# A Swin transformer block on one core: the first and last four steps ordered by hand, preparation and loads shared out anew

## The chip, the core and the metric

The kernel runs on one core of a Trainium2 chip. A core has five engines with an instruction queue of their own each: TensorE (PE, matrix products), VectorE (DVE), ScalarE (ACT), GpSimd (POOL) and SyncE (SP, here only for DMAs). They run side by side and wait for each other by semaphores. The metric is the device time of one execution in microseconds (us).

## What is computed

The reference is one Swin block on x of shape (32, 56, 56, 128) in float32: shifted windows of 7 x 7 tokens, 4 heads of 32, then an MLP with 512 hidden columns.

```python
h = roll(_ln(x, g1, b1), (-3, -3))            # then cut into windows of 49 tokens
q, k, v = split(h @ w_qkv + b_qkv)
attn = softmax(q * HD**-0.5 @ k.T + bias + MASK)
x = x + roll(window_reverse((attn @ v) @ w_proj + b_proj), (3, 3))
return x + gelu(_ln(x, g2, b2) @ w_fc1 + b_fc1) @ w_fc2 + b_fc2
```

## The kernel before

A step is 14 image rows: two bands of 8 windows, 784 tokens, held as 7 tiles of 112 tokens. An image has 4 steps, so there are 128 (`steps`). Tiles are handled in two halves, h = 0 (4 tiles) and h = 1 (3 tiles). The work of one step is spread over several turns of the loop: in turn n the kernel makes q and k of step n+1, attention and projection of step n, the hidden layer of step n-1 (`make_hidden`, 8 chunks, 0 to 3 for band 0 and 4 to 7 for band 1) and the output product of step n-2 (`make_out`).

The order is written out by hand: every engine has a function `step(n)` with its operations in a fixed order, and `run_steps` calls it for n from -3 to steps+1. `has(k)` leaves out the parts whose step does not exist, so the first and last turns keep the order of a full turn with holes in it. All waits are for semaphores that count steps.

What bears on the prediction:
- TensorE: `make_q`, `make_k`, `make_scores` (64 small products a band), `transpose_probs`, `attend`, `project`, `make_hidden` (L725 to L727, three passes), `make_out` (L767), `transpose_tiles` (L700).
- VectorE: `stats1`, `stats2`, `mean_var`, `normalise` (L530), `shift_scores` (L545 adds bias and mask, reading PSUM and writing the tile scores in SBUF; L548 takes the maximum; L550 subtracts it), `inverse_sums`, `add_to_stream` (L564: residual and final sum), `split_x` and `split_x2` (low parts).
- ScalarE: copies out of PSUM (`copy_q` L400, `copy_k`, `copy_x`, ...), `exp` (L361), `gelu` (L413). Exp and gelu need different tables, loaded by ACT_TABLE_LOAD; `load_gelu_table` (L417) loads the gelu table ahead of time with a probe of one column.
- GpSimd: `power` (rstd), `normalise_probs` (L313), `add_row` (L320: adds a bias row to the residual).
- SyncE: loads x four steps ahead, stores a step's result after both halves have their final sum.
- Preparation: weights are scaled by the layer norm's g and split in high and low parts on VectorE; TensorE makes the products of b with the weights. It is done before the first turn.

```python
283        def step(n):                                    # SyncE
290            if has(n - 2):
292                wait(sp, out_added[0], upto(n - 2))
293                wait(sp, out_added[1], upto(n - 2))
294                store((n - 2) // STEPS, (n - 2) % STEPS)
772        pe.wait_ge(front_loaded, 6 * 16)                # TensorE
```

## Time and profile before

| | us |
|---|---|
| median of 3 runs | 2976.29 (2975.44 to 2977.2) |
| the profiled execution | 2974.32 |
| its span, first to last instruction | 2972.7 |
| TensorE busy | 2932.2 (99%) |
| VectorE, ScalarE, GpSimd busy | 2578.3, 2260.8, 1299.7 |

A busy time is the sum of an engine's instructions. The granted clock is the share of full speed that TensorE had. In lists of rows, "x56" is a number of merged instructions, and "[5.03 <-DVE xn L530]" says that the engine stood idle 5.03 us before the row until that line of VectorE released it.

### The profile page before, as it was taken

Reading aid. Unit: us, or ns where it says so; the run is one execution under the profiler, and the core shown is the slowest. Engines: PE = TensorE matmul, PEld = TensorE weight load, DVE = VectorE, ACT = ScalarE, POOL = GpSimd, SP = SyncE. Lnnn points to the kernel's source line nnn. Section 1 sums busy time; section 2 is a strip of 40 time slices with the busy share of each in tenths; the row PEclk is TensorE's granted clock in tenths of the full one; section 3 lists DMA queues with packets and bytes.
Section 4 is the critical chain, followed back from the end, with each engine's and each line's share of the span. In section 5 each row is a group of like instructions: output and inputs, shape, how many; then the busy total and the mean of one; then the engine's idle time right before and its main releaser. Section 6 shows DMA issues by size and latency. Waiting matters only on the chain.

```text
span 2972.7 us, 119245 instructions
## 1 busy us (share of the span) xinstructions
PE 2932.2 (99%) x51984; PEld 2726.2 (92%) x51984; DVE 2578.3 (87%) x7463; ACT 2260.8 (76%) x4482; POOL 1299.7 (44%) x775
## 2 busy tenths in 40 slices
PE   6999999999999999999999999999999999999998
PEld 5999999999999999999999999999999999999997
DVE  7888888888888888888888888888888888888885
ACT  4777777777777777777777777777777777777775
POOL 3444444444444444444444444444444444444442
PEclk8999999999999999999999999999999999999999
DMA  2111111111111111111111111111111111111110
GB/s 52 41 35 40 35 40 35 40 37 38 37 38 40 35 40 36 41 35 40 35 40 35 40 36 40 36 39 40 35 39 37 40 35 40 35 40 35 40 24 23
DMA packets 217569, 111.77 MB, mean 38 GB/s; under 512 B 15094, under 2 KB 216790, under 8 KB 217046
## 3 DMA queue, kind: packets, MB, share of 16 engines
q1 hardware_dynamic: 215523, 103.16, 13.6%
q8 instruction: 406, 6.65, 1.0%
q10 hardware_dynamic: 1523, 1.01, 0.1%
q14 instruction: 117, 0.96, 0.1%
HBM read 52.73 MB, written 51.38 MB: 35 GB/s over the span
## 4 chain that ended last, share of the span: by engine, by line
PE 97%; DVE 2%; ACT 0%; POOL 0%; issue 0%; DMA 0%; SPq 0%; POOLq 0%; DVEq 0%
PE psum L767 26%; PE psum L725 10%; PE psum L727 8%; PE psum L726 8%; PE psum L693 7%; PE psum L746 7%; PE psum L708 7%; PE psum L753 7%; PE psum L700 6%; PE psum L732 6%; PE psum L720 6%; DVE xn L530 0%; ACT hT L413 0%; DVE row_max L548 0%; DVE scores L545 0%
## 5 line engine op out<-in xcount | busy, mean ns | idle before, releaser
L317 POOL TENSOR_TENSOR rstd<-ve,minus_half 112x7 f32<-112x7 f32 x256 | 381.1, 1489 | 1076.6 <-DVE ve L525 1076.6
L767 PEld LDWEIGHTS psum<-wfc,hT 128*112 128x112 f32 x7168 | 799.1, 177 | 38.9 <-issue 19.3
L767 PE MATMUL psum<-wfc,hT 128*112 128x128 f32 x7168 | 803.4, 273 | 1.4 <-ACT hT L413 1.4
L413 ACT ACTIVATE hT<-psum,bias_h 128x392 f32<-128x392 f32 x1024 | 575.5, 608 | 246.1 <-PE psum L727 246.1
L313 POOL TENSOR_TENSOR probs<-probs,row_inv 128x784 f32<-128x784 f32 x256 | 388.9, 1520 | 570.9 <-DVE row_inv L559 564.2
L564 DVE TENSOR_TENSOR stream<-psum,stream 112x512 f32<-112x512 f32 (+1 forms) x512 | 307.2, 609 | 204.2 <-PE psum L753 183.3
L725 PE MATMUL psum<-x2T_hi,wfc_hi 128*128 128x392 f32 x1024 | 397.2, 388 | 2.8 <-DVE x2T_lo L575 1.3
L727 PE MATMUL psum<-x2T_lo,wfc_hi 128*128 128x392 f32 x1024 | 349.3, 341 | 0.3 <-issue 0.3
L726 PE MATMUL psum<-x2T_hi,wfc_lo 128*128 128x392 f32 x1024 | 348.5, 340 | 0.1
L395 ACT ACTIVATE x2T_hi<-psum 128x336 fp32r<-128x336 f32 (+1 forms) x256 | 127.2, 497 | 254.8 <-PE psum L700 254.8
L400 ACT ACTIVATE qd<-psum,bias_q,parity_one 128x392 f32<-128x392 f32 x512 | 316.0, 667 | 5.8 <-PE psum L727 3.8
L700 PE MATMUL psum<-ident,xn 112*128 112x112 f32 x1792 | 264.6, 264 | 6.2 <-DVE xn L530 5.7
L320 POOL TENSOR_TENSOR stream<-x_in,brow_proj 112x896 f32<-112x896 f32 x128 | 269.6, 2106 | 0.0
L320 POOL TENSOR_TENSOR stream<-stream,brow_fc 112x896 f32<-112x896 f32 x128 | 268.3, 2096 | 2.0 <-DVE xn L530 2.0
L746 PE MATMUL psum<-wv,xT 128*113 128x128 f32 x2048 | 267.0, 274 | 0.0
L708 PEld LDWEIGHTS psum<-ident,probs 113*128 113x128 f32 x2048 | 218.4, 142 | 47.2 <-issue 23.6
L369 ACT ACTIVATE probsT<-psum 128x452 f32<-128x452 f32 x512 | 258.0, 572 | 0.8 <-PE psum L708 0.8
L550 DVE TENSOR_TENSOR scores<-scores,row_max 128x784 f32<-128x784 f32 x256 | 249.5, 975 | 8.7
L548 DVE TENSOR_REDUCE row_max<-scores 128x16 f32<-128x784 f32 x256 | 248.3, 970 | 8.8
L575 DVE TENSOR_TENSOR x2T_lo<-psum,x2T_hi 128x336 fp32r<-128x336 f32 (+1 forms) x256 | 143.6, 561 | 128.6 <-ACT x2T_hi L395 128.6
L746 PEld LDWEIGHTS psum<-wv,xT 128*113 128x113 f32 x2048 | 249.1, 178 | 0.0
L545 DVE TENSOR_TENSOR scores<-psum,bias_rel 128x784 f32<-128x784 f32 x256 | 246.1, 961 | 0.0
(78 smaller groups left out, 5707.3 us busy)
## 6 DMA issues: line engine op xcount, KB each, us to landing
x_in<-in_x SPq DMA_DIRECT2D x224, 168.0 KB
out<-stream SPq DMA_DIRECT2D x224, 168.0 KB
x_in<-in_x SPq DMA_DIRECT2D x224, 17.5 KB
out<-stream SPq DMA_DIRECT2D x224, 17.5 KB
x_in<-in_x SPq DMA_DIRECT2D x224, 10.5 KB
out<-stream SPq DMA_DIRECT2D x224, 10.5 KB
x_in<-in_x SPq DMA_DIRECT2D x32, 96.0 KB
out<-stream SPq DMA_DIRECT2D x32, 96.0 KB
```

Of the source, the lines that this page charges most:

```text
L313: pool.tensor_tensor(p, p, r.unsqueeze(2).to_broadcast([128, 2 * WINDOWS, N]), ALU.mult).then_inc(probs_normed[band], 1)
L317: pool.tensor_tensor(rstd[:, :], ve[:, :], minus_half[:, :], ALU.pow).then_inc(ready, 1)
L320: pool.tensor_tensor(stream[:, k % STEPS, :, :], src[:, k % STEPS, :, :], row[:, :].unsqueeze(1).to_broadcast([TOK, TILES, C]), ALU.add).t ...
L400: last = act.activation(qd[:, band, parity, :], qkvo_psum(Q_BANK[band])[:, 0:BAND], ACT.Identity, bias=bias_q[:, parity:parity + 1], scale ...
L413: act.activation(hT[:, chunk, band * BAND:(band + 1) * BAND], tok_psum(c)[:, 0:BAND], ACT.Gelu, bias=bias_h[:, chunk:chunk + 1]).then_inc( ...
L700: last = pe.transpose(tok_psum(h)[:, (t - t0) * TOK:(t - t0 + 1) * TOK], src[:, t, :], ident[0:TOK, 0:TOK])
L708: last = pe.transpose(psum[:, S_BANK + 2 * band + f, 128 * pair:128 * pair + rows], probs[0:rows, band, f, 2 * pair:2 * pair + 2, :].rearr ...
L725: pe.matmul(made, w_hi, x_hi, start=True, stop=False)
L726: pe.matmul(made, w_lo, x_hi, start=False, stop=False)
L727: return pe.matmul(made, w_hi, x_lo, start=False, stop=True)
L746: last = pe.matmul(qkvo_psum(V_BANK[band])[0:rows, pair * C:(pair + 1) * C], windows[:, 0:rows], wv[:, :], start=True, stop=True)
L767: last = pe.matmul(tok_psum(h)[0:TOK, (t - t0) * C:(t - t0 + 1) * C], hT[:, chunk, t * TOK:(t + 1) * TOK], wfc2[:, chunk, :], start=chunk ...
```

## The change

All `step(n)` functions, `has`, `fresh` and `run_steps` go. Each engine gets a straight list for steps 0 to 3, a loop `for n in range(4, steps - 4)` with the order of the old turn, and a straight list for the last four. In the new lists:
- SyncE loads x of step 0, the mask, half of the bias slices, x of step 1, then w_proj and b_proj, then x of steps 2 and 3. ScalarE's queue loads g1, b1, w_qkv, b_qkv first, then the other half of the slices, then the six MLP loads.
- GpSimd clears the padding columns of xT. VectorE clears only the padding of probs and 392 columns of the four score banks; both cleared whole tiles before.
- `make_bias_rel` is in two parts, the second behind step 3's first shift. The wfc1 split comes after `split_x(1, 1)`. The products of the biases go to banks of their own.
- `shift_scores` keeps the biased scores in PSUM, in all steps: the add writes the banks that it reads, maximum and subtraction read them.
- Scores of a step are made before the attention of the step ahead of it is finished, in the first and in the last steps.
- The last step is stored in four parts, each half as soon as its sum is there, band 0 by SyncE and band 1 by ScalarE's queue.

```diff
+        def store_last(eng, h, bands):
+            eng.wait_ge(out_added[h], steps)
+            for dst, src in token_pieces(STEPS - 1, out, images - 1, stream[:, STEPS - 1, :, :], *HALVES[h], bands):
+                eng.dma_start(dst, src).then_inc(out_stored[STEPS - 1], 16)
             load(0, 0)
-            for dst, src in ((wqkv[:, :], w_qkv), (vecs[:, 0:1], g1), (vecs[:, 1:2], b1), (bqkv[:, :], b_qkv),
-                             (wproj[:, :], w_proj), (brow_proj_in[:, :], b_proj.to_broadcast([TOK, C]))):
-                sp.dma_start(dst, src).then_inc(front_loaded, 16)
+            sp.dma_start(mask_sb[:, :, :, :], mask).then_inc(mask_loaded, 16)
             load_rel(sp, 0)
+            load(0, 1)
+            for dst, src in ((wproj[:, :], w_proj), (brow_proj_in[:, :], b_proj.to_broadcast([TOK, C]))):
+                sp.dma_start(dst, src).then_inc(proj_loaded, 16)
...
+            store_last(sp, 1, (0,))
+            store_last(sp, 0, (0,))
...
-                dve.tensor_tensor(sc, scores_psum(band), bias_rel[:, last_band, :, :, :].rearrange("p f w m -> p f (w m)"),
+                dve.tensor_tensor(made, made, bias_rel[:, last_band, :, :, :].rearrange("p f w m -> p f (w m)"),
                                   ALU.add).then_inc(scores_biased[band], 1)
...
-                dve.tensor_reduce(mx, rows, AX_X, ALU.max).then_inc(max_done[band], 1)
+                dve.tensor_reduce(mx, biased, AX_X, ALU.max).then_inc(max_done[band], 1)
...
-                dve.tensor_tensor(rows, rows, mx.unsqueeze(2).to_broadcast([128, 2 * WINDOWS, N]),
+                dve.tensor_tensor(scores[:, band, :, :, :], biased, mx.unsqueeze(3).to_broadcast([128, 2, WINDOWS, N]),
                                   ALU.subtract).then_inc(scores_shifted[band], 1)
```

TensorE's list begins:

```diff
+            make_qkv_biases()
+            pe.wait_ge(biases_ready, 1)
+            make_proj_bias()
+            pe.wait_ge(xn1_ready[0], 1)
+            transpose_tiles(xn1, 0, xT_made)
+            pe.wait_ge(xn1_ready[1], 1)
+            transpose_tiles(xn1, 1, xT_made)
+            make_hidden_biases()
...
+            make_scores(0)
...
+            make_k(0, 1)
+            make_values(0, 1)
+            pe.wait_ge(k_copied[1], 1)
+            make_k(1, 0)
+            pe.wait_ge(late_biases_ready, 1)
+            make_scores(1)
+            pe.wait_ge(k_copied[0], 2)
+            make_q(1, 0)
+            pe.wait_ge(q_copied[0], 2)
+            make_scores(0)
```

ScalarE's part up to the first exp, and VectorE's behind step 0's softmax:

```diff
+            copy_k(1)
+            act.wait_ge(k_made[0], 2)
+            copy_k(0)
+            load_gelu_table()
+            act.wait_ge(scores_shifted[0], 1)
+            exp(0)
+            act.wait_ge(q_made[0], 2)
+            copy_q(0)
...
+            inverse_sums(0, 1)
+            dve.wait_ge(scores_made[0], 2)
+            shift_scores(1, 0)
+            copy_v()
+            normalise(xn1, x_in[:, (2) % STEPS, :, :], mean1, rstd1, xn1_ready, 0)
```

TensorE's list ends, from the scores of the last step on (shortened):

```diff
+            make_scores(1)
...
+            make_hidden(2)
...
+            make_hidden(7)
+            make_values(steps - 1, 0)
...
+            make_out(0)
+            make_out(1)
...
+            attend(1)
+            pe.wait_ge(gelu_done[5], steps - 1)
+            make_hidden(7)
+            pe.wait_ge(o_copied[0], steps)
+            project(0)
+            pe.wait_ge(gelu_done[7], steps - 1)
+            project(1)
+            pe.wait_ge(residual_added[0], steps)
+            make_hidden(2)
+            pe.wait_ge(residual_added[1], steps)
+            make_out(1)
+            pe.wait_ge(gelu_done[2], steps - 1)
+            make_out(0)
...
+            make_hidden(2)
+            pe.wait_ge(gelu_done[7], steps)
+            make_out(1)
+            pe.wait_ge(gelu_done[2], steps)
+            make_out(0)
```

## Rows read from the trace of the kernel before

**Rows 1.** Stretches: length, each engine's busy time, granted clock, DMA share, GB/s.

```profile
0.00:25.00 25.00, 9.84 (x35) 6.66 (x39) 19.91 (x89) 5.94 (x12) 4.42 (x10) 1.00 0.50 118
25.00:50.00 25.00, 17.93 (x359) 15.48 (x363) 17.04 (x38) 14.40 (x27) 9.40 (x6) 0.80 0.12 34
50.00:75.00 25.00, 18.98 (x385) 16.13 (x376) 20.01 (x63) 15.62 (x31) 10.07 (x6) 0.86 0.01 2
75.00:100.00 25.00, 25.00 (x454) 23.28 (x456) 22.22 (x63) 19.88 (x40) 10.15 (x6) 1.00 0.16 42
2925.00:2973.00 48.00, 36.20 (x391) 31.99 (x389) 17.50 (x46) 17.38 (x33) 9.30 (x6) 0.98 0.11 26
```

**Rows 2.** The page: the span, and the chain that ended last by engine.

```profile
span 2972.7 us, 119245 instructions
...
PE 97%; DVE 2%; ACT 0%; POOL 0%; issue 0%; DMA 0%; SPq 0%; POOLq 0%; DVEq 0%
```

**Rows 3.** That chain in order of time: start, length, what.

```profile
5.76 5.26 DMA brow_proj_in<-in_b_proj
...
80.37 6.11 PE psum L767 x56
...
103.14 6.11 PE psum L767 x56
```

**Rows 4.** Instructions in order of time, the start: start, length, engine, line.

```profile
14.87 1.28 ACT L385 ACT_TABLE_LOAD   x1 [14.87 <-PE psum L700]
...
17.48 1.65 PE L732 MATMUL psum<-xT,wqk 128*128 128x392 f32 x2 [0.58 <-DVE brow_proj L614]
...
25.79 2.09 POOL L320 TENSOR_TENSOR stream<-x_in,brow_proj 112x896 f32<-112x896 f32 x1
...
36.90 2.99 POOL L313 TENSOR_TENSOR probs<-probs,row_inv 128x784 f32<-128x784 f32 x2 [9.02 <-DVE row_inv L559]
...
42.93 1.57 PE L720 MATMUL psum<-probsT,vs 49*32 49x49 f32 x128
...
60.02 0.82 PE L700 MATMUL psum<-ident,xn 112*128 112x112 f32 x3 [5.03 <-DVE xn L530]
...
67.27 0.43 PE L725 MATMUL psum<-x2T_hi,wfc_hi 128*128 128x392 f32 x1
```

**Rows 5.** Forms of four VectorE lines: ns of one, least/median/most, then starts.

```profile
L530 DVE TENSOR_SCALAR xn<-x_in,mean,rstd x896: 325/340/2159, 12.0 to 2892.3; 112x128 f32<-112x128 f32 x180
...
L502 DVE TENSOR_TENSOR bias_rel<-mask_sb,rel x4: 554/555/1773, 26.5 to 29.2; 128x392 f32<-128x392 f32 x4
...
L545 DVE TENSOR_TENSOR scores<-psum,bias_rel x256: 948/965/974, 29.8 to 2924.0; 128x784 f32<-128x784 f32 x128
...
L550 DVE TENSOR_TENSOR scores<-scores,row_max x256: 974/975/976, 31.8 to 2926.0; 128x784 f32<-128x784 f32 x128
```

**Rows 6.** ScalarE, 0 to 42 us, grouped by line: busy us, mean ns.

```profile
L400 ACT ACTIVATE qd<-psum,bias_q,parity_one 128x392 f32<-128x392 f32 x6 | 3.7, 670 | 4.2 <-PE psum L727 2.2 <-PE psum L732 2.0
...
L361 ACT ACTIVATE probs<-scores 128x784 f32<-128x784 f32 x2 | 1.7, 872 | 1.7 <-DVE scores L550 1.7
...
L361 ACT ACT_TABLE_LOAD x1 | 1.3, 1283 | 0.0
```

**Rows 7.** In order of time, a full step.

```profile
107.75 3.10 POOL L313 TENSOR_TENSOR probs<-probs,row_inv 128x784 f32<-128x784 f32 x2 [4.37 <-DVE row_inv L559]
...
110.06 0.94 PE L708 MATMUL psum<-ident,probs 113*128 113x113 f32 x8
```

**Rows 8.** The chain that ended last in order of time, the end.

```profile
2902.62 6.11 PE psum L767 x56
...
2954.10 0.45 PE psum L725
...
2960.68 6.38 PE psum L767 x56
2967.09 0.69 DVE stream L564
```

More of the change, by code:

```diff
@@ L51, in swin_block @@
     steps = images * STEPS
-    def has(k):
-        return 0 <= k < steps
-    def fresh(k):
-        return 0 < k < steps
     def upto(k):
         return min(k, steps - 1) + 1
-    def run_steps(step):
-        for n in range(-LEAD, steps + LAG):
-            step(n)
     with ExitStack() as ctx:
@@ L234, in v_copy, with token_pieces @@
                     qkvo_psum(V_BANK[band])[0:rows, :])
-        def token_pieces(s, dram, img, tile):
+        def token_pieces(s, dram, img, tile, lo=0, hi=WIN, bands=(0, 1)):
             pieces = []
-            for band in range(BANDS):
+            for band in bands:
                 row = STEP_ROWS * s + WIN * band + SHIFT
@@ new lines, in _ @@
+            act.wait_ge(xT_made[1], 4)
+            copy_x(3, 1)
+            act.wait_ge(fc1_made[2], 1)
+            gelu(2)
+            act.wait_ge(fc1_made[7], 1)
+            gelu(7)
+            exp(0)
+            act.wait_ge(xT_made[0], 4)
+            copy_x(3, 0)
+            act.wait_ge(xT_copied[0], 4)
+            round_x(3, 1)
+            act.wait_ge(scores_shifted[1], 3)
+            exp(1)
+            act.wait_ge(q_made[0], 4)
+            copy_q(0)
+            act.wait_ge(gelu_loaded, 3)
@@ new lines, in _ @@
+            gelu(7)
+            exp(0)
+            act.wait_ge(scores_shifted[1], 4)
+            exp(1)
+            act.wait_ge(xT_copied[0], 5)
+            round_x(4, 1)
+            act.wait_ge(q_made[0], 5)
+            copy_q(0)
+            act.wait_ge(gelu_loaded, 4)
+            load_gelu_table()
+            act.wait_ge(x2T_made[0], 3)
+            copy_x2(0)
+            act.wait_ge(k_made[0], 5)
+            copy_k(0)
+            copy_probsT(3, 1)
+            act.wait_ge(fc1_made[1], 3)
@@ new lines, in _ @@
+            copy_k(1)
+            act.wait_ge(xT_made[1], steps - 1)
+            copy_x(steps - 2, 1)
+            act.wait_ge(xT_made[0], steps - 1)
+            copy_x(steps - 2, 0)
+            act.wait_ge(fc1_made[7], steps - 4)
+            gelu(7)
+            act.wait_ge(scores_shifted[0], steps - 2)
+            exp(0)
+            act.wait_ge(xT_copied[0], steps - 1)
+            round_x(steps - 2, 1)
+            act.wait_ge(scores_shifted[1], steps - 2)
+            exp(1)
+            act.wait_ge(q_made[0], steps - 1)
@@ new lines, in _ @@
+            gelu(6)
+            copy_k(1)
+            act.wait_ge(xT_made[1], steps)
+            copy_x(steps - 1, 1)
+            copy_x(steps - 1, 0)
+            act.wait_ge(fc1_made[7], steps - 3)
+            gelu(7)
+            act.wait_ge(q_made[0], steps)
+            copy_q(0)
+            act.wait_ge(fc1_made[2], steps - 3)
+            gelu(2)
+            act.wait_ge(scores_shifted[0], steps - 1)
+            exp(0)
+            act.wait_ge(scores_shifted[1], steps - 1)
+            exp(1)
@@ new lines, in _ @@
+            load_gelu_table()
+            act.wait_ge(fc1_made[2], steps - 2)
+            gelu(2)
+            act.wait_ge(fc1_made[7], steps - 2)
+            gelu(7)
+            exp(0)
+            act.wait_ge(scores_shifted[1], steps)
+            exp(1)
+            act.wait_ge(v_made[0], steps)
+            copy_v()
+            act.wait_ge(x2T_made[0], steps - 1)
+            copy_x2(0)
+            act.wait_ge(x2T_made[1], steps - 1)
+            copy_x2(1)
+            copy_probsT(steps - 1, 0)
@@ L507, in raw_stats, with make_bias_rel @@
+            def make_bias_rel(last_band, ready):
+                if last_band == 0:
+                    dve.wait_ge(rel_loaded, 2 * WIN * 16)
+                    dve.wait_ge(mask_loaded, 16)
+                for f in range(2):
+                    last = dve.tensor_tensor(bias_rel[:, last_band, f, :, :], mask_sb[:, last_band, :, :],
+                                             rel[:, f, :].unsqueeze(1).to_broadcast([128, WINDOWS, N]), ALU.add)
+                last.then_inc(ready, 1)
             def raw_stats(src, raw, t0, t1):
@@ L886, in _, with make_qkv_biases, make_hidden_biases @@
-            run_steps(step)
+            def make_qkv_biases():
+                pe.wait_ge(front_loaded, 4 * 16)
+                for k in range(3):
+                    last = pe.matmul(psum[:, QKV_PREP_BANK, k:k + 1], wqkv[:, k * C:(k + 1) * C], vecs[:, 1:2],
+                                     start=True, stop=True)
+                last.then_inc(bias_products, 1)
+            def make_hidden_biases():
+                pe.wait_ge(back_loaded, 6 * 16)
+                for k in range(CHUNKS):
+                    last = pe.matmul(psum[:, PREP_BANK, k:k + 1], wfc1_raw[:, k * C:(k + 1) * C], vecs[:, 3:4],
+                                     start=True, stop=True)
+                last.then_inc(bias_h_products, 1)
```

1596 lines of the change are left out of this document (1266 added, 330 removed).

## The prediction

> **What bounds the kernel now.** I read four views in this order. First the stretches [rows 1]: from 75 us on TensorE is busy for the whole of each stretch, while VectorE is at 22 of 25 us. So the middle of the run is matmul work laid end to end, and nothing outside TensorE can shorten it. The idle time is at the ends: 15.2 us in the first 25, 7.1 in the second, 6.0 in the third, and 11.8 in the last 48. In the second and third stretch the granted clock is only 0.80 and 0.86, so part of what counts as busy there is the same work at the lower level (1.2 GHz). Second the chain of waits [rows 2]: 97% of it is TensorE, and in the same chain in order of time the second product of the MLP starts at 80.37 and again at 103.14 [rows 3], which gives a step of 22.77 us. All 128 steps at that pace are 2914.6 us; the span is 2972.7 [rows 2], so 58 us are what filling and draining the pipeline costs. That is all the reordering can draw on. Third, the start in order of time [rows 4]: the first projection runs at 17.48, the attention products of step 0 at 42.93, its first hidden chunk only at 67.27, and TensorE sat idle for 5.0 us just before 60.02, waiting for the normalised tokens. Fourth, the end of the chain, which is taken up below.
>
> **The change, part by part.** I cost it against the profiled execution (2974.32 us, a span of 2972.7 and 1.6 around it), and carry the difference over to the median of 2976.29.
>
> *Loads and preparation.* Before, everything early waits for the last of SyncE's six weight loads, whose wait of 5.26 us from 5.76 ends at 11.02 [rows 3]. After, the qkv weights come on ScalarE's queue in its first four DMAs, so their scaling and the first statistics can go at about 6. But TensorE's order has the projection-bias product ahead of the first transposes, and it waits for two loads that SyncE issues after 20 others (6 pieces, mask, 7 slices, 6 pieces). At the observed 0.37 to 0.45 us an issue they are out by 10 us; with the wait of the same load before, 5.3 us at most, they land between 11 and 15. I take 12.3, since the bytes ahead of them are about those that were in before at that time. The transposes then start near 12.9 instead of 13.2. The table load in front of ScalarE's first copy, 1.28 us at 14.87 [rows 4], stays behind them. The first projection, freed of the wfc1 split that held it, starts at about 16.3 instead of 17.48: 1.2 us won; 3 us lost if the load lands at 15, 1 more won if at 11. Each later microsecond moves the whole start.
>
> *The softmax of step 0.* `make_bias_rel` is halved and put ahead of the scores. Before, its four adds took 3.2 us on VectorE between the first scores and their shift; one of them took 1773 ns instead of 555 [rows 5]. So shift 0 goes some 5 us sooner. It is not kept: ScalarE's next order is both key copies, where the second waits for step 1's key product, then a gelu table load and its probe, then the exp table load (1283 ns each) and exp (872) [rows 6]. By this order exp of band 0 starts at 32.8, which is where it started before. The second scores product comes about 1 us later than before (a values product and a key product are put ahead). Adding up the copies of q (2 x 670), exp and the sums, the probabilities of the second band are normalised at 38.7, against 36.90 + 2.99 = 39.9 [rows 4]. Step 0's attention then starts near 41.9, against 42.93: 1.0 us won.
>
> *From there to the hidden layer of step 0.* Here the order changes what waits for what. Before, VectorE put both score shifts of step 1 (3 x 0.97 each) between the residual and the second normalisation, and TensorE idled. After, band 0 of step 1 is shifted while step 0's softmax runs, and only band 1 lies between. I walk the new order: residual added 49.4, statistics and rstd 53.1, shift of band 1 to 55.1, seven normalisations of 340 ns [rows 5] to 57.1 or so, transposes, copies and splits to 59.7. So the first hidden chunk is at 59.7 instead of 67.27: 7.6 us won so far, 6.5 of them here. If TensorE stays at the low clock until then, up to 2 us of it go.
>
> *To the steady loop.* The first output product follows its hidden layer by 13.1 us before (67.27 to 80.37) and 13.2 in my walk; the new one has one projection of 0.7 less ahead of it, so the comparable lead is 6.8. Then two more steps before the loop: TensorE is full before (45.5 us for two), so only losses are possible; I find 0.6 us behind the output copies in step 2 and about as much for the other gaps. Lead at the loop: 5.5 us; 3 to 10 as a range.
>
> *The score shift in PSUM, in all 128 steps.* This part isn't confined to the ends. The add now writes its PSUM source, and the maximum and the subtraction read PSUM. VectorE reads PSUM for the add at 965 ns, and SBUF alone for the subtraction at 975 [rows 5], so reading there costs nothing. No row shows a VectorE add that writes PSUM. From above it is bounded by the slack: VectorE works without a gap up to the reciprocal, GpSimd's first 1.5 us of 3.10 from 107.75 end at 109.27, and TensorE's transposes start at 110.06 [rows 7]. Six instructions can each be 0.13 us slower before TensorE waits at all. Below, 10 ns won by each is worth nothing either, since TensorE is full. I take 0.
>
> GpSimd and VectorE do get in each other's way: normalising took 2159 ns once instead of 340, and a bias add took 1773 instead of 555 beside the 2.09 us of GpSimd's add at 25.79 [rows 4, 5]. The Trainium skill ("SBUF — State Buffer", section "SBUF: two separate sides") has the rule: such a VectorE instruction, and also one with two SBUF inputs against a GpSimd one that reads SBUF, blocks for the other's whole length. By that rule the subtraction from PSUM can no longer be blocked, while each GpSimd add that the new order puts beside a normalisation or a split costs up to 2.1 us; the trace agrees on the size. In my walk one such pair lies at the end (the split of step 127 beside the add of the row), with play of about 1 us, so the cost is 0 to 1, and I take 0.
>
> *The end.* Before, TensorE goes from the query product of step 127 (0.66 us ahead of 2902.62) to the end of the last output product, 2967.05: 65.1 us [rows 8]. After, scores of step 127 are made a half step sooner, and hidden chunks and the output of step 126 fill the gaps. My walk: 22.7 us for that step, output product of 125 to 28.8, attention of 127 among the hidden chunks, with 1.1 us idle behind a gelu table load, projections at 40.4, output of 126 at 41.1 to 47.3, the last hidden chunks from 49.9. These are bound by ScalarE: 6.6 us from first chunk to output product before (2954.10 to 2960.68); here the product needs one gelu fewer, 5.9. Then 6.4 of output: 62.2. Gain 2.9, between 0 and 5.
>
> The tables there: the row says 1283 ns a load [rows 6]. The Trainium skill ("ScalarE: Activation LUTs", section "What ACT_TABLE_LOAD costs") adds a drain of about 1380 ns to each switch. The new order has about one exposed switch at either end; by that rule 2.8 us of the gain would go, by the row none. The exp that follows such a load here starts with it finished, so I stay with the row.
>
> *The last store.* Before, the last add starts at 2967.09 and takes 0.69 [rows 8], and 4.9 us follow: nine pieces issued one after another by SyncE and the landing. After, three pieces remain on either of two queues; six issues at 0.37 to 0.45 fall away, less the sharing: 1.5 us won, 0.5 to 2.5.
>
> **Sum.** 5.5 + 2.9 + 1.5 = 9.9 us. 2974.3 - 9.9 = 2964.4 in the profiled execution, 2966.4 as median.
>
> **The rivals.**
> A: the start wins far more than I walked. The idle time up to 75 us is 28 us [rows 1], and the clock adds; if the weights land by 11 and TensorE keeps the high level (2.4 GHz) from 40 us on, the lead is 12 to 16. Against it: the exp of step 0 is held by ScalarE's order, not by data. Total 17 us: 2959. Chance 0.17.
> B: the gain is eaten at the start: the projection weights land at 15 (3.9 us against my 1.2 won), and blocked normalisations take 3 more. Total 1 to 5 us won: 2973, within the band of no change. Chance 0.17.
> C, the other side: the add that writes PSUM is slower. Its point is the slack above: with six instructions on the chain to the probabilities, every 0.1 us beyond 0.13 each is 0.6 us a step, over 120 steps 72 us: 3038 at 0.23 each. At 0.15 each it is 13 us lost against 9.9 won, and there the change turns slower. For it: no row shows that write; against it: the reads cost nothing. Chance 0.06.
> D: the lag between engines at loop entry is not the one of before, and the loop settles with a small wait each step. 0.05 us a step are 6 us: 2972. Chance 0.05.
>
> **How the numbers follow.** My forecast (gain of 6.5 to 14) has 0.55. The range reaches from A's 2958 to 2973 where B and D lie, and leaves out C and the tails. What this kernel's measurement can tell from no change is about 0.2%, 6 us: faster is forecast and A and half of the rest, 0.76; same 0.18; slower 0.06.
>
> **What would show it.** In the trace after: the first projection at 16 to 17 us, and the projection-bias product waiting for its load at 12 to 13; first hidden chunk near 60; first output product near 73; loop steps still 22.77 apart; shift instructions at 0.95 to 0.98 us; from the start of the last add to the end of the span 4.1 us instead of 5.6. Wrong it is if the step differs from 22.77, if the output product of step 0 is off 73 by more than 4 us, or if the end gains less than 2.

## The result, and the profile after

| | before | after |
|---|---|---|
| median (lowest to highest), 11 executions each, same chip | 2976.75 (2974.95 to 2978.49) | 2969.45 (2966.55 to 2971.05) |
| the profiled execution | 2974.32 | 2966.55 |
| its span | 2972.7 | 2964.6 |

The change wins 7.3 us in the median: a ratio of 0.9976, with a 95% interval of 0.9966 to 0.9985. The two profiled executions lie 7.8 us apart, their spans 8.1. Forecast were 9.9. The profiled execution of the kernel after is the shortest of its eleven, 2.9 us under their median.

The stretches of the kernel after, to be held against [rows 1], with the same columns:

```profile
0.00:25.00 25.00, 8.76 (x28) 6.30 (x29) 15.56 (x85) 4.66 (x9) 4.22 (x10) 1.00 0.57 118
25.00:50.00 25.00, 19.98 (x388) 17.71 (x388) 18.95 (x38) 15.34 (x30) 11.90 (x7) 0.80 0.12 34
50.00:75.00 25.00, 22.57 (x450) 19.51 (x449) 23.93 (x78) 18.33 (x39) 9.79 (x7) 1.00 0.07 19
75.00:100.00 25.00, 23.93 (x407) 21.11 (x406) 22.07 (x64) 17.99 (x37) 8.33 (x5) 1.00 0.08 18
2925.00:2965.00 40.00, 32.74 (x351) 29.01 (x349) 12.10 (x34) 14.90 (x29) 7.98 (x5) 0.96 0.13 31
```

The third stretch has gained 3.6 us of TensorE work and the second 2.1; the first has lost 1.1, and the fourth, which was full before, has a hole of 1.1 us.

The chain that ended last, in order of time (start, length, what), for [rows 3]:

```profile
8.44 6.69 DMA brow_proj_in<-in_b_proj
15.27 0.74 PE psum L1492 x2
...
73.22 2.62 PE psum L1471 x24
...
98.59 6.11 PE psum L1471 x56
122.01 6.11 PE psum L1471 x56
```

The third output product, with which the steady pace begins, starts at 122.01; before it was 125.89 (two rows of 22.77 and 22.75 behind the 80.37 of [rows 3]). The lead at the loop is 3.9 us, not 5.5.

The same start instruction by instruction, for [rows 4]:

```profile
15.27 0.74 PE L1492 MATMUL psum<-wproj,bias_v_wide 128*112 128x128 f32 x2 [7.26 <-DMA brow_proj_in<-in_b_proj]
16.84 1.28 ACT L478 ACT_TABLE_LOAD   x1 [16.84 <-PE psum L1404]
...
31.39 0.59 ACT L498 ACTIVATE kT<-psum,bias_k 128x392 f32<-128x392 f32 x1 [1.02 <-PE psum L1436]
32.00 1.28 ACT L510 ACT_TABLE_LOAD   x1
...
33.51 1.28 ACT L454 ACT_TABLE_LOAD   x1
34.81 0.87 ACT L454 ACTIVATE probs<-scores 128x784 f32<-128x784 f32 x1
...
43.49 1.56 PE L1424 MATMUL psum<-probsT,vs 49*32 49x49 f32 x128
```

And the end, again as the chain in order of time, for [rows 8]. The query product of step 127 stands at 2896.95:

```profile
2896.95 0.66 PE psum L1436 x2
...
2938.64 6.13 PE psum L1471 x56
...
2947.43 0.45 PE psum L1429
...
2954.38 6.15 PE psum L1471 x56
2960.53 0.02 issue
2960.56 0.69 DVE stream L1032
```

From the start of the last add to the end of the span it is 4.04 us (2964.6 - 2960.56); before it was 5.61.

So the 8.1 us between the spans split into 3.9 at the start, 0.6 over the 120 turns between the output products of steps 2 and 122 (125.89 to 2856.71 before, 122.01 to 2852.25 after), 0.5 from there to the query product of step 127 (45.24 us before, 44.70 after), 1.5 from it to the last output (65.1 before, 63.6 after) and 1.6 in the store. The 0.6 can't be put down to the change: traces with the same loop differ by up to 3 us over these 120 turns (last section).

### The profile page after: what moved, and what is told of

The parts are those of the page before. It is cut to its first block, busy times and chain, and to the rows that moved or that the text cites. A ratio compares the mean times of both kernels' runs of the same rounds, so it can differ in the third digit from the quotient of the medians.

```text
span 2964.6 us, 119363 instructions
## 1 busy us (share of the span) xinstructions
PE 2932.3 (99%) x51984; PEld 2726.4 (92%) x51984; DVE 2572.8 (87%) x7462; ACT 2258.3 (76%) x4480; POOL 1300.0 (44%) x776
## 4 chain that ended last, share of the span: by engine, by line
PE 98%; ACT 1%; DVE 0%; SPq 0%; DMA 0%; issue 0%; DVEq 0%; ACTq 0%
PE psum L1471 26%; PE psum L1429 10%; PE psum L1431 8%; PE psum L1430 8%; PE psum L1397 8%; PE psum L1450 7%; PE psum L1412 7%; PE psum L1457 7%; PE psum L1404 6%; PE psum L1436 6%; PE psum L1424 6%; DMA brow_proj_in<-in_b_proj 0%; ACT qd L493 0%; ACT hT L506 0%; ACT oT L469 0%; SPq L275 0%
## 5 line engine op out<-in xcount | busy, mean ns | idle before, releaser
L1016 DVE TENSOR_REDUCE row_max<-psum 128x16 f32<-128x784 f32 x256 | 249.5, 974 | 8.8
L1018 DVE TENSOR_TENSOR scores<-psum,row_max 128x784 f32<-128x784 f32 x256 | 249.4, 974 | 8.8
L1013 DVE TENSOR_TENSOR psum<-psum,bias_rel 128x784 f32<-128x784 f32 x256 | 248.7, 971 | 4.5 <-PE psum L1397 4.4
L1397 PEld LDWEIGHTS psum<-kT,qd 64*49 64x49 f32 x16384 | 212.6, 123 | 42.0 <-ACT qd L493 4.4
```

Of the source, the lines that this page charges most:

```text
L1397: last = pe.matmul(scores_psum(band)[half:half + N, f, cols], qd[rows, band, parity, cols], kT[rows, band, cols], start=True, stop=True)
```

## The experiments

"After" below is the changed kernel. All medians have a run of the kernel before beside them on the same chip, and chips differ by up to 1.6 us in it (2975.19 to 2976.79), so ratios are compared. An *anchor* is the start of an instruction in the profiled execution.

### The two halves alone, and two single parts

e5_new_head_alone: every engine's list for the first four steps, loads and preparation are the new ones; from step 4 the old turn goes on to the end, and the store is the old one. The score shift in PSUM stays.

```
-for n in range(4, steps - 4): ...   # and the new list of the last four
+def step(n): ...                    # the old turn, has(k) and all
+for n in range(4, steps + 2): step(n)
```

> New order for steps 0 to 3, then the old turns to the end and the old store. Theory: head and tail add up independently. The head's lead at the first output product of the loop is that of the changed kernel, 3.9 us (122.0 against 125.9), and the end is that of before (65.1 us from the last band-0 query product to the last output product's end, 5.6 us from there to the end of the span): span 2968 to 2969, ratio about 0.9987. Rival (settling): the loop with the old tail drifts back to the old phase and the lead is gone before the end: span 2972 to 2973.

e6_new_tail_alone: the old start and old turns up to step 123, then the new lists and the new last store.

```
-for n in range(-LEAD, steps + LAG): step(n)
+for n in range(-LEAD, steps - 4): step(n)
+...                                 # the new list of the last four
```

> Old preparation, old order and scores in SBUF up to step 123, then the new lists of the last four and the store in four parts. Theory: 1.3 us from the order of the last turns, 0.4 to 0.7 from the turns before them, 1.6 from the store, so the span is 2969 to 2969.5, ratio about 0.9988. The low clock in the last run of hidden chunks shows here too (6.8 us from first chunk to output product, at 0.33 us a pass for some of them). Rival: that low clock belongs to the changed kernel's history and not to its end, then 5.9 us and a span of 2968.5.

Measured: the head alone 2972.09 us (ratio 0.9986, 0.9977 to 0.9994), the tail alone 2974.09 (0.9991, 0.9982 to 1.0), 4.2 and 2.2 us won beside their own run of before. Together 6.3 against 7.3 for both at once: the parts add up within what these medians can tell. From the output product of step 122 to the end of the span the old tail takes 116.0 us in before and 116.1 behind the new head, the new one 112.4 in after and 113.8 behind the old head. The start earns what it earns without the tail.

Two things in these traces were not expected. The third output product of e5 stands at 119.53, a lead of 6.4 us and not 3.9, with the same instruction lists up to there as in after. Two more kernels with these lists, e4 and e7 below, have it at 119.94 and 120.82. So the lead of the new start is 3.9 to 6.4 us by trace, and after's own trace is the low end.

And the new tail is 1.4 us dearer behind the old start because e6 keeps the old score shift, in all steps. Its chain runs through one subtraction of 2.54 us, and from the output product of step 122 to that of step 124 it takes 47.14 us instead of 45.89. e3, the next experiment, which has the new start and the old shift, takes 47.15. The last product is another 0.2 longer (6.34 us instead of 6.15).

e3_scores_in_sbuf puts the old score shift into after:

```
-dve.tensor_tensor(made, made, bias_rel..., ALU.add)
+dve.tensor_tensor(sc, scores_psum(band), bias_rel..., ALU.add)
-dve.tensor_reduce(mx, biased, AX_X, ALU.max)
+dve.tensor_reduce(mx, rows, AX_X, ALU.max)      # rows: the SBUF tile
-dve.tensor_tensor(scores[...], biased, mx..., ALU.subtract)
+dve.tensor_tensor(rows, rows, mx..., ALU.subtract)
```

> The changed kernel with the score shift of before (the add writes the tile in SBUF). Theory: VectorE is off the path and its times are the same (971 against 961 ns for the add), so span and anchors stay: first output product 73.2, step 22.75, end 2964.6 within 0.3 us. Rival by the port rule: with two SBUF inputs the subtraction can now be blocked by a GpSimd instruction; in the start two adds of GpSimd (26.9 to 31.1) lie beside the subtraction at 29.5, which then takes 2.5 us instead of 0.97, and the second shift follows later or not (it waits for its scores until 32.3): 0 to 0.3 us.

Measured: 2969.43 (0.9978, 0.9968 to 0.9987) beside after's 0.9976: nothing, as forecast. The anchors did not stay, though (first output product at 71.91 instead of 73.22, end of the span at 2966.6 instead of 2964.6), and in the traces the shift does cost something. All 256 of each form, ns of one as least/median/most, after first:

```profile
L1013 DVE TENSOR_TENSOR psum<-psum,bias_rel x256: 957/974/983, 27.5 to 2918.3; 128x784 f32<-128x784 f32 x128
...
L1018 DVE TENSOR_TENSOR scores<-psum,row_max x256: 974/974/975, 29.5 to 2920.3; 128x784 f32<-128x784 f32 x128
```

and e3:

```profile
L1013 DVE TENSOR_TENSOR scores<-psum,bias_rel x256: 910/966/975, 27.6 to 2921.1; 128x784 f32<-128x784 f32 x128
...
L1018 DVE TENSOR_TENSOR scores<-scores,row_max x256: 974/975/2543, 29.6 to 2923.1; 128x784 f32<-128x784 f32 x128
```

The add that writes PSUM costs 8 ns more than the one that writes SBUF. The other end of the row is the surprise: inside SBUF one subtraction took 2543 ns, from PSUM none took more than 975. In e3 the 10 subtractions of the first 130 us average 1217 ns and the 12 of the last 167 us 1106, the 234 between them 975. So the port rule that the prediction weighed shows in this pair: with the score tile in SBUF the hand-made order has three lengthened subtractions in the start and one in the end, some 2.4 and 1.6 us of VectorE's time, and with it in PSUM none. The one in the end beside GpSimd's add, in e3:

```profile
2874.62 2.09 POOL L329 TENSOR_TENSOR stream<-stream,brow_fc 112x896 f32<-112x896 f32 x1
...
2875.00 2.54 DVE L1018 TENSOR_TENSOR scores<-scores,row_max 128x784 f32<-128x784 f32 x1
```

and the same pair in after:

```profile
2873.07 2.09 POOL L329 TENSOR_TENSOR stream<-stream,brow_fc 112x896 f32<-112x896 f32 x1
...
2873.46 0.97 DVE L1018 TENSOR_TENSOR scores<-psum,row_max 128x784 f32<-128x784 f32 x1
```

In e3 and in e6 this subtraction lies on the chain that ended last, and the stretch around it is 1.25 us longer than in after (above). So keeping the scores in PSUM is worth 1.25 us of the new tail. The median does not show it.

e4_store_whole undoes the last store alone:

```
-store_last(sp, 1, (0,)); store_last(sp, 0, (0,))     # and ScalarE's two
+sp.wait_ge(out_added[1], steps); sp.wait_ge(out_added[0], steps)
+store(images - 1, STEPS - 1)
```

> The new kernel with one thing undone: the last store is again made by SyncE alone, in nine pieces after both halves have their final sum. My theory of the last store: from the start of the last add to the end of the span 5.6 us as before, against 4.04 in the new kernel; the median 1.5 us above the new kernel's 2969.45, so 2971. Rival: the order in which the last halves end matters too (the first half's pieces are on their way while TensorE still works), which the stretch from the last add shows as well; or the landing of one DMA is all that counts: 4.1 to 4.5, time 2969.5.

Its instructions at the end:

```profile
2959.15 0.69 DVE L1030 TENSOR_TENSOR stream<-psum,stream 112x512 f32<-112x512 f32 x1 [2.94 <-PE psum L1469]
2959.91 3.29 SPq L279 DMA_DIRECT2D out<-stream  x9
```

The span is 2964.7, so 5.55 us from the start of the last add, against 4.04 in after: 1.5 for this store, as in the theory. The median does not show it: 2966.58, a ratio of 0.9972 (0.9961 to 0.9982) that lies even below after's, inside its interval. 1.5 us are 0.05%, a quarter of the width of such an interval; and this execution's start was 2.1 us ahead of after's with the same lists (output product of step 2 at 119.94), which goes with its clock (last section). The size of the store's gain rests on the traces alone, but there it is steady: 4.0 to 4.1 us in every trace with the new store, 5.55 to 5.61 in the three with the old one.

### What held the start

e1_proj_bias_later moves TensorE's projection-bias product, which waits for the load, behind the first projection, and the hidden-bias products behind the first key product. It also lets the first query product start with the scaled weights, where after waits for their low parts too (shortened):

```
 make_qkv_biases()
-pe.wait_ge(biases_ready, 1)
-make_proj_bias()
 pe.wait_ge(xn1_ready[0], 1)
 ...
-make_hidden_biases()
+pe.wait_ge(biases_ready, 1)
+pe.wait_ge(qkv_scaled, 1)
 pe.wait_ge(xT_copied[1], 1)
-pe.wait_ge(wqk_ready, 1)
 make_q(0, 0)
+make_proj_bias()
 ...
 make_k(0, 0)
+make_hidden_biases()
+pe.wait_ge(wqk_ready, 1)
```

> In the changed kernel TensorE makes the projection-bias product behind the first query product and the hidden-bias products behind the first key product, and the first query product waits only for the scaled weights. Theory (the landing of w_proj and b_proj at 15.1 set the start): the first projection goes from 19.20 to 15.0 to 15.5; of its 4 us 1 is lost to the two bias products in the chain, the first output product is at 70 to 71 instead of 73.2, and the span falls by 2.5 to 3.5 us. Rival: the start is held by something that comes after anyway (x of step 1 lands at 13.9, its statistics and normalisation, or the table loads at 32.0): the first projection is earlier, the first exp (34.81) moves less than 1 us, and the span stays.

Measured: 2963.15 (0.9957, 0.9945 to 0.997). In its trace the first transposes go at 12.09, with the tokens, not with the load:

```profile
12.09 1.01 PE L1404 MATMUL psum<-ident,xn 112*128 112x112 f32 x4 [3.82 <-DVE xn L998]
...
15.65 1.64 PE L1436 MATMUL psum<-xT,wqk 128*128 128x392 f32 x2 [1.05 <-ACT xT L478]
```

The first projection is 3.55 us sooner than in after, exp 2.3, step 0's attention 3.1, its first hidden chunk 4.2 (55.84), the third output product 4.05 (117.96). Against all four traces with after's start lists the third output product is 1.6 to 4.05 us sooner. The median is 13.1 us under before's on the same chip, 5.8 more than after's, and each of e1's five executions is shorter than each of after's eleven. That is more than the 2.5 to 3.5 us expected, and more than the anchors show; the rest I can't place. What held the start was the wait on the load in TensorE's order, with two smaller things behind it that the same edit removed: the wait for the low parts, which end at 16.16 in e1's trace, 0.5 us behind its first projection, and the hidden-bias products (1.7 us). The three were not tried one by one.

e2_no_first_probe leaves out the first gelu table load with its probe, which stood in front of the first exp; only the counts of the later probes' semaphore move with it.

```
 copy_k(0)
-load_gelu_table()
 act.wait_ge(scores_shifted[0], 1)
```

> The changed kernel without the first load_gelu_table (between the key copy of step 1 and the first exp). Theory: the chain of the start goes through ScalarE's gelu table load, probe and exp table load (32.0 to 34.8), so the first exp starts 1.5 us sooner, at 33.3, the attention of step 0 at 42.0 instead of 43.5 and the first output product about 1.5 us sooner; median 1 to 1.5 us lower. Rival: exp of band 1 waits for its shift (ends 35.3) and the chain changes to VectorE, then the first exp moves but the attention only 0.3 us, and the span stays.

Measured: 2970.03 (0.9977, 0.9968 to 0.9987). Both loads of 1.28 us vanish (the table load at 16.17 is then the only one up to 45 us), and exp runs at 31.73 instead of 34.81, 3.1 us sooner where 1.5 were expected. Attention still starts at 43.41 (43.49 in after) and the loop is no sooner (122.66). e8_later_and_no_probe is both edits together:

> Both start edits together: the bias products behind the first query and key products, and no first gelu probe. Theory (one chain through both): the gains add up, the first projection at 15.7, the first exp at 31.0, first output product at 67.5 to 68, median 1 to 1.5 us below the kernel with the first edit alone (2963.2). Rival: VectorE, which works without a gap from 35 to 55 us in that kernel, has become the chain, and the probe gives less than 0.5.

Measured: 2966.96 (0.9968, 0.9955 to 0.998), not better than e1 alone. Exp is at 28.94, 3.5 us ahead of e1, attention at 40.63 against e1's 40.40, the first hidden chunk at 57.27 against 55.84. The stretches of e8 show where it may have gone:

```profile
30.00:35.00 5.00, 2.91 (x74) 2.64 (x74) 4.90 (x9) 2.12 (x3) 0.62 (x1) 0.83 0.29 80
35.00:40.00 5.00, 3.27 (x18) 2.95 (x17) 4.90 (x11) 2.14 (x5) 2.37 (x2) 0.50 0.00 0
40.00:45.00 5.00, 3.88 (x137) 3.39 (x136) 4.41 (x13) 3.33 (x10) 1.18 (x1) 0.50 0.02 5
```

and of e1:

```profile
30.00:35.00 5.00, 1.23 (x30) 0.60 (x34) 4.80 (x8) 4.96 (x7) 0.01 (x1) 0.97 0.25 74
35.00:40.00 5.00, 4.70 (x74) 4.38 (x68) 4.62 (x7) 1.84 (x5) 3.02 (x2) 0.69 0.02 5
40.00:45.00 5.00, 3.73 (x146) 3.31 (x145) 4.90 (x16) 4.11 (x12) 0.65 (x1) 1.00 0.02 3
```

The first number behind the length is TensorE's busy time, the third from the end the granted clock. In e8 TensorE is at the lower level (0.50, 1.2 GHz) for ten microseconds; in e1 it is back at 2.4 GHz from 40. In both VectorE is busy for 4.4 to 4.9 of 5 us up to 45. That suggests two chains beside each other, VectorE's and that of a TensorE at half speed, of which a sooner exp shortens neither. It is not shown: 1.4 us at an anchor are less than the difference between traces of one and the same list (table below).

Three kernels on top of e1 probe these two. e9_late_and_split_sooner prepares w_fc1 on VectorE between the two score shifts of step 0 instead of behind the splits of step 1:

```
 shift_scores(0, 0)
+split_fc1_weights()
 dve.wait_ge(scores_made[1], 1)
 ...
 split_x(1, 1)
-split_fc1_weights()
```

> The new kernel with the projection-bias product behind the first band's products (as in e1_proj_bias_later, 2963.15 us) and, in addition, VectorE's preparation of w_fc1 (scaling, high part, low part: 0.48 + 0.43 + 0.69 = 1.6 us at 41.44 in the trace of e1) put between the two score shifts of step 0, where VectorE stands idle 2.40 us before 29.98. My theory: from 35 to 50 us VectorE is the chain of the start, so 1.6 us taken out of it there bring step 0's first hidden chunk from 55.84 to 54.2 and the loop anchor from 117.96 to about 116.4; time 2961.5. Rival 1: TensorE's level decides, since it stood idle more; the hidden chunk stays at 55.5 to 56, time 2963. Rival 2, the other side: the six MLP loads are not in at 28 and the second shift waits for them: exp of band 0 behind it late by 1 to 3 us, time 2965.

e10_late_and_filled fills TensorE's wait ahead of the scores of step 1:

```
 make_q(1, 0)
+for _ in range(24):
+    pe.matmul(tok_psum(1)[:, 0:C], wqk[:, 0, :], wqk[:, 0, :], start=True, stop=True)
 pe.wait_ge(q_copied[0], 2)
```

> e1_proj_bias_later with 24 products of 128 columns that nobody uses, put on TensorE ahead of the step-1 scores of band 0, where it stood idle for 3.77 us before 34.53. In e1 the granted clock fell to 0.69 in the stretch 35 to 40 behind that idle time. Theory of the clock: with the time filled TensorE keeps the level of 2.4 GHz in 35 to 40 (granted clock 0.9 or more), the 72 products from 34.53 and the values take 0.5 to 1.0 us less, of which up to 0.8 arrives at the first hidden chunk (55.0 instead of 55.84); time 2962.4. Rival: VectorE is the chain in that stretch, TensorE's level there changes nothing: hidden chunk at 55.6 to 56, time 2963 within 0.6. Other side: 24 products at the lower level take 2.6 us or more and push the scores: at most 0.5 us lost.

e11_late_split_filled has both:

> Both together: projection-bias product later, w_fc1 prepared between the two score shifts, 24 unused products before the step-1 scores. If VectorE's chain sets the start and the clock is second, the two add up: first hidden chunk at 53.5 to 54.2, loop anchor near 116, time 2960.7. If only the split counts, as e9_late_and_split_sooner. If neither, 2963.

| anchors, us | first exp | attention 0 | hidden chunk 0 | output product 2 | median | ratio |
|---|---|---|---|---|---|---|
| after | 34.81 | 43.49 | 60.07 | 122.01 | 2969.45 | 0.9976 |
| e4, after's start | 34.54 | 42.94 | 57.90 | 119.94 | 2966.58 | 0.9972 |
| e5, after's start | 33.66 | 41.90 | 57.02 | 119.53 | 2972.09 | 0.9986 |
| e7, after's start | 35.30 | 43.22 | 58.66 | 120.82 | 2969.25 | 0.9974 |
| e1 | 32.48 | 40.40 | 55.84 | 117.96 | 2963.15 | 0.9957 |
| e8 | 28.94 | 40.63 | 57.27 | 119.40 | 2966.96 | 0.9968 |
| e9 | 31.57 | 40.40 | 55.40 | 117.41 | 2962.98 | 0.9959 |
| e12, e9's start | 31.21 | 41.01 | 55.99 | 118.17 | 2963.87 | 0.9961 |
| e10 | 32.08 | 40.65 | 57.17 | 118.66 | 2963.66 | 0.9960 |
| e11 | 31.33 | 39.95 | 54.90 | 116.25 | 2963.64 | 0.9959 |

The four traces with one start differ by up to 3.1 us at the hidden chunk and 2.5 at the output product, so only e1's step away from all four is clear; the differences among e1, e8, e9, e10 and e12 at these two anchors are not.

My theory for e9 failed in size: 0.44 us sooner at the hidden chunk, not 1.6, and e12, with the same start lists, is 0.15 later than e1. Exp was 0.9 sooner, attention not at all (40.40 in both), with the granted clock at 0.75 and 0.56 from 30 to 40, lower than in e1. In e10 the fill did hold the level from 30 to 40:

```profile
30.00:35.00 5.00, 5.00 (x45) 4.86 (x44) 4.54 (x9) 4.80 (x7) 0.41 (x1) 1.00 0.27 77
35.00:40.00 5.00, 4.06 (x93) 3.60 (x92) 4.36 (x6) 1.89 (x4) 2.63 (x2) 1.00 0.01 2
40.00:45.00 5.00, 3.74 (x143) 3.35 (x142) 4.90 (x15) 3.64 (x11) 0.40 (x1) 0.90 0.01 3
45.00:50.00 5.00, 5.00 (x91) 4.83 (x89) 3.95 (x19) 1.74 (x5) 3.16 (x2) 0.75 0.14 40
```

but the scores of step 1 moved from 34.53 to 35.65, and the lower level came at 45 to 50 instead. The hidden chunk is 1.3 us later than in e1: the case I had called the other side, only dearer. With both edits (e11) the clock was 1.00 in every stretch up to 60, and attention, hidden chunk and output product are the earliest of all; the start is 1.7 us ahead of e1's, with the anchor that was expected (116). The expected time (2960.7) did not come: that is the profiled execution (2960.51), the shortest of five, and the median is 2963.64. Medians can't separate e1, e9, e10, e11 and e12.

### The end

e7_filled_end puts 4 and 10 products that nobody uses into the two waits ahead of the last hidden run:

```
 transpose_tiles(xn2, 1, x2T_made)
+for _ in range(4): pe.matmul(psum[:, PREP_BANK, 0:C], wproj, wproj)
 pe.wait_ge(out_added[0], steps - 1)
 transpose_tiles(xn2, 0, x2T_made)
+for _ in range(10): pe.matmul(psum[:, PREP_BANK, 0:C], wproj, wproj)
 pe.wait_ge(x2T_split[0], steps)
 make_hidden(1)
```

> The changed kernel with 4 and 10 products of 128 x 128 without use, into a free bank, in TensorE's two waits ahead of the last step's hidden chunks (0.49 and 1.3 us). Theory: the low clock in that run (0.33 us a pass for half of it, 15.74 us from the output product of step 126 to that of step 127 in some runs, 14.73 in others) comes after the idle time, so filling it gives 14.7 always, and the median falls by 0.5 to 1 us. Rival: the clock falls for another reason (the power level, a fixed time), then both lengths still occur, and the extra products cost up to 0.3 us.

e12_short_fill has 2 and 5 of them, on top of e9:

> e9_late_and_split_sooner with 2 + 5 products of 128 columns that nobody uses in the two waits ahead of the last hidden run (0.49 and 1.29 us idle in the new kernel). In e7_filled_end, 4 + 10 such products kept the granted clock at 1.00 there and the run from its first chunk to the output product took 5.89 us instead of 6.95, but they ended 0.9 us after the split that they should only have waited for. Theory of the clock at the end: with half as many, the level of 2.4 GHz stays and the start of the run is not pushed: output product of step 126 to that of step 127 takes 14.7 to 14.9 instead of 15.74, and the median is 0.9 us under e9's 2962.98: 2962.1. Rival: half the fill doesn't hold the level, granted clock 0.75 to 0.88 in the last hidden run as without any; 15.6 to 15.8, time 2963. Other side: the products still push the transposes or the chunks by some 0.3 us each and the level falls as well: 16.1, 2963.4.

After's instructions there, a pass at the lower level and one at the higher:

```profile
2947.43 0.45 PE L1429 MATMUL psum<-x2T_hi,wfc_hi 128*128 128x392 f32 x1 [1.29 <-DVE x2T_lo L1043]
...
2948.60 0.53 PE L1430 MATMUL psum<-x2T_hi,wfc_lo 128*128 128x392 f32 x1
...
2952.39 0.34 PE L1430 MATMUL psum<-x2T_hi,wfc_lo 128*128 128x392 f32 x1
```

Its run from first chunk to output product takes 6.95 us (2947.43 to 2954.38). In e7 the second and third passes are all at 0.33 to 0.34 and the run takes 5.89, but the ten products take 2.41 us where 1.29 were idle, and the chunks start 9.7 us behind the output product of step 126 instead of 8.8: 15.59 us from output product to output product instead of 15.74, and a median of 2969.25 (0.9974), where 0.5 to 1 us less than after's were expected. In e12 the chain reads

```profile
2936.75 6.11 PE psum L1471 x56
...
2945.54 0.45 PE psum L1429
...
2951.47 6.38 PE psum L1471 x56
```

14.72 us, one less than in e9 (15.74), as the theory of the clock had it. The median is 2963.87 (0.9961, 0.9947 to 0.9975), 1.8 above the forecast, and can't show it. Nor is the fill proved to be what kept the level: of the ten traces with this tail and no fill, seven have a granted clock of 0.75 in the run, but e1, e3 and e11 kept the higher level and took 14.73 us each. Shown is what the level is worth, 1.0 us in the run, of which the last output product gives some back in after (6.15 us against 6.38 in e1); what decides whether it falls in a given execution is open.

## Why the prediction was nearly right

The forecast case came true in its bounds (a gain of 6.5 to 14: 7.3 measured), 2.6 us short of its centre. In part that is luck: the load landed outside my range for it, and a walk that was too slow made up for it. Its terms:

**The load, mis-sized.** I took 12.3 for the landing of the projection weights and 11 to 15 as the range; TensorE got going at 15.27, just past the late end. The issue was right (8.44), but this load then took 6.7 us where the same one took 5.26 before [rows 3]: I had counted the bytes ahead of it as equal. They were not: up to the landing the core moved 172 GB/s before (11.02 us) and 175 after (15.13 us), some 1.9 MB against 2.6. The rate was about the same, and more had been moved by the time it landed. The first projection came at 19.20 instead of 16.3, and 1.7 later than before instead of 1.2 sooner. That is rival B's condition. Its price was too high by my own walk: a landing at 15 instead of 12.3 puts the projection at 19.0, 1.5 us later than before, not 3, and 2.7 behind my centre, not 3.9. The other half of B, blocked normalisations, did not come: the normalisations of the first 100 us average 341 ns, and the four bias adds are at 555 each, none at 1773 [rows 5].

**The walk from there, too pessimistic.** The first projection is 2.9 us late by my walk, exp 2.0, attention 1.6, the first hidden chunk 0.4 (60.07 for 59.7), the first output product 0.3 (73.22 for 72.9). So 2.6 us of my walk between the projection and the output product were not there. I take it that I had laid waits of one engine behind waits of another that ran side by side; no run separates them. Two errors cancelled: e4, e5 and e7, with the same lists, have the first output product at 71.07, 70.59 and 71.82, and without them and e1 one would take the 73 for a confirmed walk. After's own 73.22 goes with a low clock, 0.62 to 0.69 from 35 to 50, for which I had named up to 2 us and put none into the sum.

**From first output to the loop, mis-sized.** Two steps took 45.5 us before. They take 48.79, 3.3 more, and in e1, e3, e4, e5 and e7 48.9 to 49.2. I had allowed for 0.7 of one projection more and some 1.3 of gaps. TensorE's busy time in the two steps of after:

```profile
73.22:98.59 25.37, 24.30 (x411) 21.48 (x410) 22.40 (x63) 18.36 (x38) 7.63 (x6) 1.00 0.08 18
98.59:122.01 23.42, 23.42 (x408) 21.32 (x408) 18.31 (x56) 18.55 (x36) 12.47 (x8) 1.00 0.21 54
```

It is idle for 1.07 us in the first step and for nothing in the second, so the gaps were sized well. The chain names ScalarE's work as it goes by, but TensorE waits little for it:

```profile
90.66 0.59 ACT hT L506
91.25 1.21 ACT qd L493 x2
```

TensorE's own instructions at that time:

```profile
91.54 0.82 PE L1457 MATMUL psum<-wproj,oT 128*112 128x128 f32 x6
92.50 0.44 PE L1429 MATMUL psum<-xT_hi,wqk_hi 128*128 128x392 f32 x1
```

Behind the gelu and the query copy it stood still for 0.15 us; the larger holes are 0.35 at 87.09 and 0.43 in front of 88.96, the projection behind ScalarE's output copies, which I had found. The term that I had at nothing is TensorE's own time: it is busy for 47.7 us where two steps took 45.5, at a granted clock of 1.00. Two more query products account for 0.7 of it. The rest, 1.5 us, is the same number of products in another order, 0.7 of it in the second step, which has no hole at all. Why they take longer in that order no run shows.

So the lead at the loop came out at 3.9 us in after and at 5.1 to 6.4 in e7, e4 and e5, around my 5.5: with the first output product 1.1 to 2.3 us ahead of my walk there, and some 1.4 more than I allowed lost behind it.

**PSUM, right in the loop, mis-sized at the end.** 974 ns each for the add and the subtraction, the turn unchanged at 22.75 in both traces, and e3's median equal. Rivals C and D fall with it. But I put the part at nothing everywhere, and at the end it is worth the 1.25 us that e3 and e6 lose there.

**The port rule, right, and the pair that I had named without weight.** I had one pair in the walk, the split of step 127 beside GpSimd's add:

```profile
2908.65 4.49 POOL L329 TENSOR_TENSOR stream<-x_in,brow_proj 112x896 f32<-112x896 f32 x2
2908.97 2.22 DVE L1039 TENSOR_TENSOR xT_lo<-xT,xT_hi 128x392 fp32r<-128x392 f32 x1
```

The split took 2.22 us instead of 0.56, and so the rule of the Trainium skill ("SBUF — State Buffer", section "SBUF: two separate sides") holds here to its size. Nothing on the chain waited for it. The other half of what I took from the rule, that a subtraction from PSUM is no longer blocked, e3 bears out (975 ns at most against 2543). e9 met it as well: the scaling of w_fc1 took 1.37 us beside a GpSimd add, 0.48 elsewhere.

**The tables, right.** The row's price was right and the page's drain absent: in after the load at 32.00 follows a copy that ends at 31.98, and exp at 34.81 follows a load that ends at 34.79. The Trainium skill ("ScalarE: Activation LUTs", section "What ACT_TABLE_LOAD costs") would have 1.38 us more at each; the measurement decides.

**The end, mis-sized.** 62.2 us were forecast from the query product to the end of the last output, 63.6 measured: a gain of 1.5 instead of 2.9. By this trace the output product of step 126 came at 41.7 instead of 41.1, the last hidden run at 50.5 (forecast 49.9), and took 6.95 instead of 5.9 at the lower level; the last product was 0.2 shorter. By my own test (wrong if the end gains less than 2) this step failed, though 0.5 us, which I had not looked for, were won in the turns just ahead. With the level kept, e1 takes 5.93 for the run, my 5.9, and 62.8 us from the query product to the end of the last output (2895.93 to 2958.72): a gain of 2.3, inside the test. So the lower level explains 0.8 of the missing 1.4 us, and the later output product the rest.

**The store, right.** 1.57 us against 1.5, and e4 confirms it (5.55 us without it, 4.04 with it).

So in after's trace 3.9 + 1.5 + 1.6 stand against 5.5 + 2.9 + 1.5; 0.5 us more came from the turns just ahead of the last query product, which I had put at zero, and 0.6 from the loop, within what traces of the same loop differ by. The 2.6 us by which the median falls short can't be split among the terms more finely than that.

## What to carry to other kernels

Before a reordering is costed, look in every engine's list for the first instruction that waits for a late load, and count what is queued behind it: here one bias product, whose result VectorE reads at 21.92 in e1, held the whole start: moved, with what stood behind it, it gives 1.6 to 4.05 us at the loop and 5.8 in the median, where the whole new start alone had won 4.2. Walk the first steps behind a pipeline's fill with the same care as the fill, since a full engine before says nothing about the holes that a new order opens, nor about how long the same products take in it. Where the chain names another engine, look at how long the bounding one really stood idle (0.15 us here, beside 1.8 us of ScalarE's work in the chain). And where TensorE falls idle for a few microseconds in a fill or drain, allow for its clock: the same list reached the loop up to 2.5 us sooner or later, and its granted clock differed with it, so one profile of one version does not rank two orders that differ by less.

## What the runs showed of the hardware

- The same 120 turns took 2733.3 us in e1's trace, 2730.2 in after's, 2732.7 in e3's. The difference is spread over the whole loop: the median turn is 22.75 us in seven of the fourteen traces and 22.77 in six (22.76 in e12), at a granted clock of 1.00 between 200 and 2800 us in all. It does not follow the kernel: before has the one and e6, with the same loop, the other. Some 2 us of a profiled execution's span come from this; its cause is open.
- In the same list the higher level came back at different times: in after the granted clock is 0.69 and 0.66 in 40:45 and 45:50, in e4 0.78 and 1.00, in e7 0.97 and 1.00, in e5 0.90 and 1.00. The third output product came at 122.01, 119.94, 120.82 and 119.53.
- With a fill of unused products the level held where it was put (1.00 from 30 to 40 in e10, against 0.97 and 0.69 in e1), and it fell later all the same (0.75 from 45 to 50); in e11, with the same fill, it did not fall.
- VectorE's subtraction of 128x784 took 974 to 975 ns from PSUM beside a GpSimd add, and up to 2543 inside SBUF beside the same add (e3, e6).
